# Attention and FFN block: norms and residual moved to GpSimd, the bias of every head pair copied into PSUM

## The chip, the cores and the metric

The kernel runs on one core of a Trainium2 chip. The metric is the device time of one execution in microseconds, median of the runs. Engines are called TensorE (PE in the rows; PEld is its weight load), VectorE (DVE), ScalarE (ACT), GpSimd (POOL) and SyncE (SP, which issues DMAs).

## What is computed

Input x is 8 batches of 256 tokens of 128 features, float32. Layer norms have no gain or shift, eps is 1e-5.

```python
x = x + _layernorm(attn(_layernorm(x)))
x = x + _layernorm(ffn(_layernorm(x)))

def attn(x):                       # 16 heads of 8
    qkv = x @ W_qkv + b_qkv
    ...
    scores = einsum('bihd,bjhd->bhij', q, k) / sqrt(8)
    rel = clip(idxs[:, None] - idxs[None, :] + 128, 0, 256)
    scores = scores + transpose(rel_bias[rel], (2, 0, 1))[None]
    out = einsum('bhij,bjhd->bihd', softmax(scores), v)
    return out @ W_out + b_out

def ffn(x):                        # 128 -> 512 -> 512 -> 512 -> 128, ternary weights, per-output scales
    h = silu(x @ w1 * s1) * (x @ w2 * s2)
    h = gelu(h @ h1 * h1s); h = gelu(h @ h2 * h2s)
    return h @ w3 * w3s
```

## The kernel before

**Number format.** TensorE works in float32r, which keeps fewer bits than float32. Where that matters an operand is split in a high part (rounded) and a low part (the rest), and products of both are added. The table of relative biases lies in SBUF as `raw` (128 x 16 heads x 384, so that every head's bias of a tile is a window), its rounded form as `table_hi`, and for one pair of heads also the rest, `table_lo`.

**Program.** It is written by hand in one queue per engine, with semaphores; nothing is reordered. There are 8 pairs of heads (s = 0 to 7) in each of 8 batches (b = 0 to 7). Token tiles of 128 come in five units of 2, 2, 4, 4 and 4; each unit is normalised (`x_moments`, `inv_std` on GpSimd, `x_normalize`), transposed (`x_T`) and multiplied with the weights of q, k and v (`q_and_k`, `v`).

**Softmax.** The maximum of a row must be known before the exponential. So each pair is multiplied twice: once one batch ahead for the maximum (`max_scores` L1222, 4 matmuls; `max_bias` L1240, 2 matmuls with the identity that add `table_hi`; `maxima` L683 on VectorE), and once transposed for the probabilities (`scores` L1257, 4 matmuls, which also subtract the maximum by an extra row). The bias of this second product is in PSUM before the scores are added: `write_bias` copies the windows of `raw` there, on ScalarE (L1012) for pairs 0, 1, 3, 4, 6, on VectorE (L690) for pairs 2 and 5 (`BY_DVE`). In the last batch VectorE takes 1, 2, 4, 5, 6. For pair 7 (`BY_PE`) nobody copies: `score_bias` (L1276) adds `table_hi` and `table_lo` with 4 matmuls behind the scores. ScalarE's `probabilities` (L1004) is the exponential, and `weighted` (L1285) multiplies two pairs with v. Three PSUM places of two banks rotate: pair i of the scores and pair i of the maxima use place i % 3, so a bias may be written only when `maxima` has read the place (`ms_read`), and a maximum's matmuls may start only when the exponential has read it (`exp_done`).

**The steps of a batch.** In step s of batch b TensorE does the scores of (b, s), the maximum's product of (b+1, s), its bias, for s = 7 the bias matmuls, and then one of the small things for batch b-1: `back` (s 1, 2: weighted heads back to tokens), `heads_T` (s 3), `project` (s 4, L1317: the output projection, P below) and `norm_T` (s 7, L1324: transposes the second norm z into the FFN's input, N below). In step 6 of batches 1 to 4 it also does unit 4's transpose or products, ahead of the maximum's product.

**The norms around the attention**, all of batch b-1 during batch b. VectorE: `attn_moments` (s 4, L709: adds b_out, statistics of y), `residual` (s 5, L719: normalises y in two instructions, adds it to xs, statistics of the sum), `second_norm` (s 6, L731: normalises into z in two instructions), `z_low` (s 7, L739). GpSimd computes each reciprocal root (`inv_std` L514), and between the batches it splits the FFN's weights into parts (`split_weights`, four instructions of 128 x 512 a piece, up to three pieces a batch, L559 to L571).

```python
if s == 5:
    residual(b - 1)
if s == 6:
    second_norm(b - 1)
```

**The FFN** (`ffn`, L1542) follows in four chunks of 512 tokens. Its first part contains the rest of batch 7: `back`, `heads_T`, `project`, and `norm_T(B - 1)` ahead of the last outputs of `layer2`. GpSimd, VectorE and ScalarE split the activations into parts.

Of the kernel before, what the change touches and what calls it, by code (L numbers as in the profile page):

```python
# [4 lines left out]
F32 = mybir.dt.float32  # L5
# [9 lines left out]
P = 128  # L15
# [42 lines left out]
BY_PE = (7,)  # L58
BY_DVE = (2, 5)
LAST_BY_DVE = (1, 2, 4, 5, 6)  # L60
LOW_AT_SLOT = {2 * s + k: 2 * i + k for i, s in enumerate(BY_PE) for k in range(2)}
# [25 lines left out]
def build(nc, x, wq, wk, wv, bqk, brows, bv, wo, bo, ext, w1, s1, w2, s2, h1, h1s, h2, h2s, w3, w3s,  # L87
          ident_in, out):
    ctx = ExitStack()
    with ctx:  # L90
# [49 lines left out]
        rows_at = lo_at + 2 * len(BY_PE) * WIN  # L140
        room = sb("room", [P, max(rows_at + 4 * PAIRS * S, 2 * NK * CH * SLOTS)], F32R)
        table_hi = room[:, hi_at:lo_at].rearrange("p (h c) -> p h c", h=H)
        table_lo = room[:, lo_at:rows_at].rearrange("p (h c) -> p h c", h=2 * len(BY_PE))
# [97 lines left out]
        table_lo_set = sem("table_lo_set")  # L241
# [103 lines left out]
        def by_act(b):  # L345
            return tuple(s for s in range(PAIRS) if s not in BY_PE + by_dve(b))

# [158 lines left out]
        def _(pool):  # L506
# [20 lines left out]

            x_inv_std(0)
# [3 lines left out]
            x_inv_std(1)  # L532
            x_inv_std(2)
            for s in range(PAIRS):
                table_high(s)
                if s == 5:
                    x_inv_std(3)
            for i, s in enumerate(BY_PE):
                pool.wait_ge(table_hi_pool, s + 1)
                nc.gpsimd.tensor_tensor(table_lo[:, 2 * i:2 * i + 2, :], raw[:, 2 * s:2 * s + 2, :],  # L540
                                        table_hi[:, 2 * s:2 * s + 2, :].bitcast(F32),
                                        ALU.subtract).then_inc(table_lo_set, 1)

            x_inv_std(4)

# [48 lines left out]
            inv_std((B - 1) * 2 + NU + 1, TPB)  # L594
            inv_std((B - 1) * 2 + NU + 2, TPB)
# [7 lines left out]
        def _(dve):  # L603
# [24 lines left out]
            def x_normalize(u):  # L628
                first, tiles = UNITS[u]
                dve.wait_ge(rstd_set, u + 1)  # L630
                if u >= 3:
                    dve.wait_ge(xnT_ready, 2 if u == 3 else 4)
# [28 lines left out]
            x_moments(1)  # L661
# [3 lines left out]
            spread_weights(nc.vector.tensor_copy, 0, (0,))  # L665
            dve.wait_ge(brows_in, 16)
# [6 lines left out]
            x_normalize(1)  # L673
            dve.wait_ge(ident_loaded, 16)
            nc.vector.tensor_scalar(minus_ident[:, :], ident[:, :], -1.0, None, ALU.mult).then_inc(minus_set, 1)
            dve.wait_ge(qk_w_in[2], 16)
# [32 lines left out]
            def attn_moments(b):  # L709
# [6 lines left out]
                dve.wait_ge(y_read, b + 1)  # L716
# [937 lines left out]
```

## Time and profile before

| | us |
|---|---|
| median of 3 runs (lowest, highest) | 291.42 (290.83, 292.56) |
| profiled execution: its time | 292.18 |
| profiled execution: span of the profile | 290.4 |

| engine | busy us | share of the span |
|---|---|---|
| TensorE | 268.5 | 92% |
| VectorE | 219.3 | 76% |
| ScalarE | 205.9 | 71% |
| GpSimd | 102.4 | 35% |

The granted clock of TensorE is full in all but the last stretch (mean 0.991). The span can be read in four parts: loading, first norms and the maxima of batch 0 (to 33 us), batches 0 to 6 (to 178), the last batch (to 194), and the FFN (to the end). A busy TensorE does not mean a TensorE at its peak: the duration of a matmul in the rows overlaps the next one's, so costs are taken from start to start.

### The profile page before, as it was taken

The page shows a single profiled execution, that of the slowest core. Times are in us where ns is not written, and L with a number is a line of the kernel's source. Part 1 is how long each engine was busy: PE and PEld are TensorE (multiplying, and loading weights), DVE is VectorE, ACT ScalarE, POOL GpSimd, SP SyncE. Part 2 cuts the span into 40 slices and gives each one's busy share as a digit, 9 for nine tenths or more (in the row PEclk, how much of TensorE's full clock was granted, in tenths as well). Part 3 has the DMA queues.
Part 4 walks back from the last instruction along what each step waited for, and adds up shares of the span by engine and source line. Part 5 has one row for each costly group of instructions (what it writes and reads, how often), then busy time and mean ns, then how long its engine had stood idle before and what let it go on. Part 6 is the DMA issues. An engine that isn't in the chain of part 4 may idle for free.

```text
span 290.4 us, 5171 instructions
## 1 busy us (share of the span) xinstructions
PE 268.5 (92%) x1875; PEld 180.4 (62%) x1875; DVE 219.3 (76%) x442; ACT 205.9 (71%) x316; POOL 102.4 (35%) x107
## 2 busy tenths in 40 slices
PE   7999989899999999999998998899999999999980
PEld 7756645555555554565554554567887888888860
DVE  3489977889789889889889899848556843673674
ACT  2777777776786786885886876777469976896750
POOL 7616000103504305906966957018630202400111
PEclk9999999999999999999999999999999999999996
DMA  6979506232221263470320200000000000010012
GB/s 166 320 238 142 184 11 208 89 83 77 74 76 38 77 207 124 138 224 8 104 81 19 61 1 3 1 3 1 0 2 0 0 0 2 0 36 2 2 36 77
DMA packets 21356, 21.17 MB, mean 73 GB/s; under 512 B 3664, under 2 KB 18768, under 8 KB 21072
## 3 DMA queue, kind: packets, MB, share of 16 engines
q1 hardware_dynamic: 20464, 20.53, 24.8%
q8 instruction: 17, 0.28, 0.4%
q10 hardware_dynamic: 864, 0.27, 0.4%
q14 instruction: 11, 0.09, 0.1%
HBM read 14.90 MB, written 5.64 MB: 71 GB/s over the span
## 4 chain that ended last, share of the span: by engine, by line
PE 60%; DVE 22%; ACT 9%; issue 5%; DMA 1%; POOL 0%; SPq 0%; ACTq 0%; DVEq 0%
PE place L1441 10%; PE place L1442 10%; PE place L1244 8%; DVE mx L685 7%; PE pv L1296 6%; PE place L1236 4%; ACT ring L1008 4%; DVE y_and_z L620 4%; PE place L1270 4%; DVE stats L609 2%; PE place L1195 2%; DVE place L692 2%; ACT place L1015 2%; PE pv L1442 2%; PE pv L1441 2%
## 5 line engine op out<-in xcount | busy, mean ns | idle before, releaser
L685 DVE TENSOR_REDUCE mx<-place 128x4 f32<-128x1024 f32 x64 | 78.1, 1222 | 13.1 <-PE place L1244 11.8
L517 POOL TENSOR_TENSOR rstd<-mv,mhalf 128x2 f32<-128x2 f32 (+1 forms) x26 | 21.0, 809 | 153.0 <-DVE mv L617 153.0
L1008 ACT ACTIVATE ring<-place 128x1024 f32<-128x1024 f32 x64 | 65.6, 1027 | 6.3 <-PE place L1281 3.0
L1244 PE MATMUL place<-room,identr 128*128 128x512 f32 x128 | 46.9, 447 | 0.0
L1015 ACT COPY place<-raw 128x1024 f32<-128x1024 f32 x37 | 37.7, 1022 | 12.2 <-DVE mx L685 11.9
L1441 PE MATMUL place<-room,w_hi 128*128 128x512 f32 (+1 forms) x116 | 44.6, 387 | 0.7 <-DVE room L818 0.7
L1442 PE MATMUL place<-room,w_hi 128*128 128x512 f32 (+1 forms) x116 | 44.0, 382 | 0.0
L818 DVE TENSOR_TENSOR room<-ring,room 128x512 fp32r<-128x512 f32 x32 | 21.4, 690 | 18.5 <-ACT room L1096 18.5
L1296 PE MATMUL pv<-ring,vx 128*9 128x256 f32 x512 | 33.6, 380 | 0.0
L1270 PE MATMUL place<-room 33*128 33x256 f32 x256 | 31.7, 328 | 1.1 <-DVE place L692 1.0
L1236 PE MATMUL place<-room 33*128 33x256 f32 x256 | 28.3, 297 | 2.9 <-ACT ring L1008 2.7
L1270 PEld LDWEIGHTS place<-room 33*128 33x128 f32 x256 | 18.9, 184 | 15.4 <-issue 12.2
L1020 ACT COPY oT<-pv 128x256 f32<-128x256 f32 x32 | 11.8, 370 | 22.2 <-PE pv L1296 22.1
L1236 PEld LDWEIGHTS place<-room 33*128 33x128 f32 x256 | 19.8, 185 | 10.1 <-issue 6.8
L1441 PEld LDWEIGHTS place<-room,w_hi 128*128 128x128 f32 x116 | 21.8, 188 | 5.1 <-DVE room L818 0.9
L1244 PEld LDWEIGHTS place<-room,identr 128*128 128x128 f32 x128 | 19.0, 188 | 8.6
L1442 PEld LDWEIGHTS place<-room,w_hi 128*128 128x128 f32 x116 | 21.8, 188 | 4.1
L692 DVE COPY place<-raw 128x1024 f32<-128x1024 f32 x19 | 23.2, 1225 | 0.6
L1094 ACT ACTIVATE ring<-place,hs 128x512 f32<-128x512 f32 x27 | 18.5, 686 | 5.9 <-PE place L1442 5.9
L1296 PEld LDWEIGHTS pv<-ring,vx 128*9 128x9 f32 x512 | 10.9, 90 | 17.3 <-issue 9.9
L830 DVE SCALAR_TENSOR_TENSOR ring<-place,hs,raw 128x512 f32<-128x512 f32 x16 | 12.0, 750 | 12.0 <-ACT raw L1073 11.8
L1096 ACT CAST room<-ring 128x512 fp32r<-128x512 f32 x32 | 19.9, 621 | 1.0
(141 smaller groups left out, 442.9 us busy)
## 6 DMA issues: line engine op xcount, KB each, us to landing
raw<-ext SPq DMA_DIRECT2D x8, 384.0 KB, 6.9
room<-q_parts SPq DMA_DIRECT2D x48, 64.0 KB
room<-k_parts SPq DMA_DIRECT2D x48, 64.0 KB
w_lo<-h SPq DMA_DIRECT2D x2, 1024.0 KB, 5.2
q_parts<-w_hi SPq DMA_DIRECT2D x4, 256.0 KB, 3.0
k_parts<-w_hi SPq DMA_DIRECT2D x2, 512.0 KB, 3.4
xs<-x SPq DMA_DIRECT2D x3, 256.0 KB, 5.7
w_lo<-w SPq DMA_DIRECT2D x3, 256.0 KB, 2.7
```

The source lines that it names most:

```text
L517: nc.gpsimd.tensor_tensor(rstd[:, at:at + width], mv[:, at:at + width, 1], mhalf[:, 0:width], ALU.pow).then_inc(rstd_set, 1)
L685: nc.vector.tensor_reduce(mx[:, s // RPAIRS, :, :, s % RPAIRS].rearrange("p i k -> p k i"), max_tile(b * PAIRS + s)[:, :, :].rearrange("p ...
L692: nc.vector.tensor_copy(score_tile(i)[:, :, :].rearrange("p k (j n) -> p k j n", j=2), pair_windows(raw[:, :, :], i % PAIRS)).then_inc(bia ...
L818: nc.vector.tensor_tensor(lo, act_f[:, half[c], k, :], hi.bitcast(F32), ALU.subtract).then_inc((a1_lo_set, a2_lo_set)[i], 1)
L1008: nc.scalar.activation(probs[:, s % PRING, :, :, :].rearrange("p k j n -> p (k j n)"), score_tile(b * PAIRS + s)[:, :, :].rearrange("p k n ...
L1015: nc.scalar.copy(score_tile(i)[:, :, :].rearrange("p k (j n) -> p k j n", j=2), pair_windows(raw[:, :, :], i % PAIRS)).then_inc(bias_set, 1)
L1236: mm(max_tile(b * PAIRS + s)[:, half, it * S:(it + 1) * S], rows(q_rows, b, half, s)[:, it * P:(it + 1) * P], rows(k_rows, b, half, s), st ...
L1244: last = mm(max_tile(b * PAIRS + s)[:, half, :], identr[:, :], windows(table_hi[:, 2 * s + half, :], 0, P, 2, S), start=False, stop=True, ...
L1270: last = mm(tile[:, half, j * S:(j + 1) * S], rows(k_rows, b, half, s)[:, j * P:(j + 1) * P], rows(q_rows, b, half, s), start=(s in BY_PE ...
L1296: last = mm(pv[32 * r:32 * r + VC, 0:S], vx[:, b * TPB + j, 4 * g + r, :], probs[:, (2 * g + r // 2) % PRING, r % 2, j, :], start=(j == 0) ...
L1441: mm(o, w, hi, start=first, stop=False)
L1442: done = mm(o, w, lo, start=False, stop=last and exact)
```

## The change

- **Bias.** `BY_PE` and `score_bias` are gone. Pair 7's bias is copied like the others, by VectorE in batches 0 to 6 (`BY_DVE` is 2, 5, 7; written in step 5), by ScalarE in the last batch. `table_lo` is not computed. `table_hi` stays for the maxima.
- **Norms.** GpSimd does `residual` and `second_norm` of every batch, the statistics of the sum stay on VectorE as `x1_moments`, in step 6. GpSimd also normalises units 2, 3 and 4 of x, between the casts of the table.
- **Start.** The moments of unit 1 come behind the normalising of unit 0.
- **FFN.** `project(B - 1)` follows output 2 of `layer1` of chunk 1, where it followed output 1.

```diff
-BY_PE = (7,)
-BY_DVE = (2, 5)
+BY_DVE = (2, 5, 7)
...
@@ GpSimd
+            def residual(b):
+                inv_std(b * 2 + NU + 1, TPB)
+                pool.wait_ge(rstd_set, b * 2 + NU + 1)
+                for t in range(TPB):
+                    last = normalize(y[:, t, :], y[:, t, :], t)
+                last.then_inc(y_norm, 1)
+                pool.wait_ge(y_norm, b + 1)
+                xb = xs[:, TPB * b:TPB * b + TPB, :]
+                nc.gpsimd.tensor_tensor(xb, xb, y[:, :, :], ALU.add).then_inc(x1_set, 1)
+
+            def second_norm(b):
+                inv_std(b * 2 + NU + 2, TPB)
+                pool.wait_ge(rstd_set, b * 2 + NU + 2)
+                if b > 0:
+                    pool.wait_ge(zT_ready, b)
+                for t in range(TPB):
+                    last = normalize(z[:, t, :], xs[:, b * TPB + t, :], t)
+                last.then_inc(z_set, 1)
...
+            table_high(0)
+            table_high(1)
             x_inv_std(2)
-            for s in range(PAIRS):
+            table_high(2)
+            x_normalize(2)
+            for s in range(3, 6):
                 table_high(s)
-                if s == 5:
-                    x_inv_std(3)
-            for i, s in enumerate(BY_PE):
-                pool.wait_ge(table_hi_pool, s + 1)
-                nc.gpsimd.tensor_tensor(table_lo[:, 2 * i:2 * i + 2, :], raw[:, 2 * s:2 * s + 2, :],
...
+            x_inv_std(3)
+            x_normalize(3)
+            table_high(6)
+            table_high(7)
             x_inv_std(4)
+            x_normalize(4)
...
                 if b > 0:
-                    inv_std((b - 1) * 2 + NU + 1, TPB)
-                    inv_std((b - 1) * 2 + NU + 2, TPB)
+                    residual(b - 1)
+                    second_norm(b - 1)
                 for piece in SPLIT_AT[b]:
                     split_weights(piece)
...
@@ VectorE
             x_moments(0)
             dve.wait_ge(qk_w_in[0], 16)
             nc.vector.tensor_scalar(wq_sb[:, :], wq_sb[:, :], scale, None, ALU.mult).then_inc(bq_scaled, 1)
-            x_moments(1)
             x_normalize(0)
             dve.wait_ge(row_zeros, 1)
             dve.wait_ge(bq_scaled, 1)
             spread_weights(nc.vector.tensor_copy, 0, (0,))
+            x_moments(1)
...
-                        if s == 5:
-                            residual(b - 1)
                         if s == 6:
-                            second_norm(b - 1)
+                            x1_moments(b - 1)
...
@@ TensorE
-                    if s in BY_PE and more:
-                        score_bias(b, s)
-                    if s + 1 in BY_PE and not more:
+                    if s + 2 == PAIRS and not more:
 
                         scores(b, s + 1)
-                        score_bias(b, s + 1)
...
-                whole(layer1, 1, exact, (0, 1))
+                whole(layer1, 1, exact, (0, 1, 2))
                 project(B - 1)
-                whole(layer1, 1, exact, (2, 3))
+                whole(layer1, 1, exact, (3,))
```

VectorE's queue in batch 6, from the moments of y to the low part of z, before (`mx<-place` are the maxima of pairs 5, 6 and 7 of the next batch; `y_and_z` is y in the first two rows and z in the last two of it):

```order
L617 TENSOR_SCALAR mv<-mv 128x2 [waits dve_order]
L685 TENSOR_REDUCE mx<-place 128x2x2 [waits ms_ready]
L620 TENSOR_SCALAR y_and_z<-y_and_z,mv,rstd 128x128 [waits rstd_set]
L727 TENSOR_TENSOR xs<-xs,y_and_z 128x256 [waits y_norm]
L609 BN_STATS stats<-xs 128x6 [waits x1_set]
L685 TENSOR_REDUCE mx<-place 128x2x2 [waits ms_ready]
L620 TENSOR_SCALAR y_and_z<-xs,mv,rstd 128x128 [waits zT_ready,rstd_set]
L743 TENSOR_TENSOR z_parts<-misc,z_parts 128x256 [waits z_hi_set]
```

and after:

```order
L646 TENSOR_SCALAR mv<-mv 128x2 [waits dve_order]
L712 TENSOR_REDUCE mx<-place 128x2x2 [waits ms_ready]
L719 COPY place<-raw 128x1024 [waits ms_read]
L712 TENSOR_REDUCE mx<-place 128x2x2 [waits ms_ready]
L638 BN_STATS stats<-xs 128x6 [waits x1_set]
L712 TENSOR_REDUCE mx<-place 128x2x2 [waits ms_ready]
L758 TENSOR_TENSOR z_parts<-misc,z_parts 128x256 [waits z_hi_set]
```

The bias of pair 7 (`place<-raw`) has come in behind the maxima of pair 5, and the statistics of the sum, which stood ahead of the maxima of pair 6, stand behind them; both normalisings and the addition have left.

GpSimd's queue between two batches' weight pieces, after (before, only the two `rstd` rows stood there):

```order
L513 TENSOR_TENSOR rstd<-mv,mhalf 128x2 [waits var_set]
L525 TENSOR_SCALAR y_and_z<-y_and_z,mv,rstd 128x128 [waits rstd_set]
L545 TENSOR_TENSOR xs<-xs,y_and_z 128x256 [waits y_norm]
L525 TENSOR_SCALAR y_and_z<-xs,mv,rstd 128x128 [waits zT_ready,rstd_set]
L588 CAST w_hi<-w_lo 128x512 [waits parts_out4,ffn_w_in3]
```

The weight pieces of a batch now stand behind five more instructions.

TensorE's queue in step 7 of a batch, before:

```order
L1270 MATMUL place<-room 128x256 [waits ms_read]
L1236 MATMUL place<-room 128x256 [waits exp_done]
L1244 MATMUL place<-room,identr 128x512 x2
L1281 MATMUL place<-room,identr 128x512 x4
L1327 MATMUL misc<-ident,y_and_z 128x128 [waits z_set,mrow_set]
```

and after:

```order
L1275 MATMUL place<-room 128x256 [waits bias_set_dve]
L1243 MATMUL place<-room 128x256 [waits exp_done]
L1251 MATMUL place<-room,identr 128x512 x2
L1322 MATMUL misc<-ident,y_and_z 128x128 [waits z_set,mrow_set]
L1275 MATMUL place<-room 128x256 [waits bias_set,mrow_in0]
```

Between the bias of the maxima and the transpose of z the four matmuls are gone; the scores of pair 7 now wait for VectorE's copy.

## Rows read from the trace of the kernel before

**Rows 1.** The page, part 1: busy us, share of the span, instructions.
```profile
PE 268.5 (92%) x1875; PEld 180.4 (62%) x1875; DVE 219.3 (76%) x442; ACT 205.9 (71%) x316; POOL 102.4 (35%) x107
```

**Rows 2.** TensorE's timeline, batches 1 and 2: start, us, what, [idle before].
```profile
65.55 0.71 PE L1320 MATMUL misc<-wo_sb,onT 128*128 128x128 f32 x4
...
69.56 0.74 PE L1244 MATMUL place<-room,identr 128*128 128x512 f32 x2
...
73.40 0.38 PE L1327 MATMUL misc<-ident,y_and_z 128*128 128x128 f32 x2
...
86.17 0.71 PE L1320 MATMUL misc<-wo_sb,onT 128*128 128x128 f32 x4
...
90.67 0.73 PE L1244 MATMUL place<-room,identr 128*128 128x512 f32 x2
...
94.99 0.44 PE L1327 MATMUL misc<-ident,y_and_z 128*128 128x128 f32 x2 [0.35 <-DVE w_hi L640]
...
107.26 0.71 PE L1320 MATMUL misc<-wo_sb,onT 128*128 128x128 f32 x4
```

**Rows 3.** TensorE's timeline, batch 5: projection, bias matmuls, transpose, next projection.
```profile
149.46 0.71 PE L1320 MATMUL misc<-wo_sb,onT 128*128 128x128 f32 x4
...
155.53 1.09 PE L1281 MATMUL place<-room,identr 128*128 128x512 f32 x4
...
157.68 0.41 PE L1327 MATMUL misc<-ident,y_and_z 128*128 128x128 f32 x2 [1.06 <-DVE y_and_z L620]
...
169.67 0.71 PE L1320 MATMUL misc<-wo_sb,onT 128*128 128x128 f32 x4
```

**Rows 4.** VectorE's timeline over the same part of batch 5.
```profile
147.81 1.23 DVE L692 COPY place<-raw 128x1024 f32<-128x1024 f32 x1
...
151.54 1.22 DVE L685 TENSOR_REDUCE mx<-place 128x4 f32<-128x1024 f32 x1
...
152.68 0.60 DVE L620 TENSOR_SCALAR y_and_z<-y_and_z,mv,rstd 128x128 f32<-128x128 f32 x2
...
153.77 0.49 DVE L609 BATCH_NORM_STATS2 stats<-xs 128x6 f32<-128x128 f32 x2
...
154.65 1.22 DVE L685 TENSOR_REDUCE mx<-place 128x4 f32<-128x1024 f32 x1
...
155.78 1.74 DVE L620 TENSOR_SCALAR y_and_z<-xs,mv,rstd 128x128 f32<-128x128 f32 x2
```

**Rows 5.** GpSimd's timeline, batch 5: the root of the second norm.
```profile
154.82 0.70 POOL L517 TENSOR_TENSOR rstd<-mv,mhalf 128x2 f32<-128x2 f32 x1 [2.38 <-DVE mv L617]
```

**Rows 6.** GpSimd's groups by line and shape: busy us, mean ns of one, idle before.
```profile
L569 POOL TENSOR_SCALAR w_hi<-w_lo 128x512 fp32r<-128x512 f32 x10 | 15.0, 1505 | 0.9
...
L561 POOL TENSOR_TENSOR w_lo<-w_lo,w_hi 128x512 f32<-128x512 f32 x11 | 14.1, 1284 | 0.9
...
L559 POOL CAST w_hi<-w_lo 128x512 fp32r<-128x512 f32 x11 | 6.8, 620 | 0.0
...
L525 POOL CAST room<-raw 128x768 fp32r<-128x768 f32 x8 | 6.3, 830 | 0.9 <-DMA raw<-ext 0.9
...
L540 POOL TENSOR_TENSOR room<-raw,room 128x768 fp32r<-128x768 f32 x1 | 1.8, 1809 | 0.1
```

**Rows 7.** TensorE's timeline: start, end of batch 0, last batch, FFN.
```profile
7.31 0.41 PE L1169 MATMUL misc<-ident,xn 128*128 128x128 f32 x2 [0.80 <-DVE xn L620]
...
54.12 0.51 PE L1236 MATMUL place<-room 33*128 33x256 f32 x4 [0.77 <-ACT ring L1008]
...
190.73 1.05 PE L1296 MATMUL pv<-ring,vx 128*9 128x256 f32 x16
...
220.12 0.71 PE L1320 MATMUL misc<-wo_sb,onT 128*128 128x128 f32 x4 [0.69 <-ACT onT L1024]
```

**Rows 8.** ScalarE's timeline, last batch.
```profile
189.00 1.94 ACT L1008 ACTIVATE ring<-place 128x1024 f32<-128x1024 f32 x2 [1.57 <-PE place L1270]
```

More of the change, by code:

```diff
@@ L55 @@
 SLOT_HEAD = [s + HALF * k for s in range(PAIRS) for k in range(2)]
-BY_PE = (7,)
-BY_DVE = (2, 5)
+BY_DVE = (2, 5, 7)
 LAST_BY_DVE = (1, 2, 4, 5, 6)
-LOW_AT_SLOT = {2 * s + k: 2 * i + k for i, s in enumerate(BY_PE) for k in range(2)}
 def windows(ap, start, step, count, width):
@@ L345, in by_act @@
         def by_act(b):
-            return tuple(s for s in range(PAIRS) if s not in BY_PE + by_dve(b))
+            return tuple(s for s in range(PAIRS) if s not in by_dve(b))
         BLANKS = (2, 2, 2, 6, 6)
@@ L526, in table_high, with normalize, x_normalize @@
                                       raw[:, 2 * s:2 * s + 2, :]).then_inc(table_hi_pool, 1)
+            def normalize(dst, src, t, at=0):
+                return nc.gpsimd.tensor_scalar(dst, src, mv[:, at + t, 0:1], rstd[:, at + t:at + t + 1],
+                                               ALU.subtract, ALU.mult)
+            def x_normalize(u):
+                first, tiles = UNITS[u]
+                pool.wait_ge(rstd_set, u + 1)
+                if u >= 3:
+                    pool.wait_ge(xnT_ready, 2 if u == 3 else 4)
+                for t in range(tiles):
+                    last = normalize(x_norm[u][:, t, :], xs[:, first + t, :], t, first)
+                last.then_inc(xn_set, 1)
+            def residual(b):
[15 more added lines that the diff above has]
+                last.then_inc(z_set, 1)
             x_inv_std(0)
@@ L593, in _ @@
             gate_parts(2)
-            inv_std((B - 1) * 2 + NU + 1, TPB)
-            inv_std((B - 1) * 2 + NU + 2, TPB)
+            residual(B - 1)
+            second_norm(B - 1)
             gate_parts(3)
@@ L716, in attn_moments, with x1_moments @@
                 dve.wait_ge(y_read, b + 1)
+                if b > 0:
+                    dve.wait_ge(z_set, b)
                 moments(lambda t: y[:, t, :], TPB, b * 6 + base + 2)
[L719 to L727 removed]
+            def x1_moments(b):
                 dve.wait_ge(x1_set, b + 1)
                 moments(lambda t: xs[:, b * TPB + t, :], TPB, b * 6 + base + 4)
[L731 to L737 removed]
             def z_low(b):
@@ L748, in _ @@
                 if s == 0:
-                    x_normalize(2)
                     keep_v(0)
@@ L863, in _ @@
             layer_low(1, 0, (0, 1))
-            residual(B - 1)
+            x1_moments(B - 1)
             layer_low(1, 0, (2, 3))
-            second_norm(B - 1)
             layer_low(0, 1)
@@ L1271, in scores @@
                                   rows(k_rows, b, half, s)[:, j * P:(j + 1) * P], rows(q_rows, b, half, s),
-                                  start=(s in BY_PE and j == 0), stop=False, skip_group_check=True)
-                if s not in BY_PE:
-                    last.then_inc(st_ready, 1)
-            def score_bias(b, s):
-                if b == 0:
-                    pe.wait_ge(table_lo_set, BY_PE.index(s) + 1)
-                for half in range(2):
-                    for part in (table_hi[:, 2 * s + half, :], table_lo[:, LOW_AT_SLOT[2 * s + half], :]):
-                        last = mm(score_tile(b * PAIRS + s)[:, half, :], identr[:, :], windows(part, 0, P, 2, S),
-                                  start=False, stop=True, skip_group_check=True)
+                                  start=False, stop=False, skip_group_check=True)
                 last.then_inc(st_ready, 1)
@@ L1356, in _ @@
                 for s in range(PAIRS):
-                    if more or s not in BY_PE:
+                    if more or s < PAIRS - 1:
                         scores(b, s)
```

33 lines of the change are left out of this document (3 added, 30 removed).

## The prediction

> **What bounds the kernel now.** I read the page's busy shares first, then TensorE's timeline around the eight attention batches, then VectorE's and GpSimd's over the same stretch, and last the groups of GpSimd instructions. TensorE is busy for 92% of the span [rows 1], so the first question is whether the bias matmuls of pair 7, which the change removes from it, stand where TensorE has no slack. They don't. In batch 5 the last thing before the transpose of the second norm (L1327) is the group of four bias matmuls at 155.53 (1.09 us, of which the last 0.1 overlap, so about 0.95 of path), and then the transpose waits 1.06 us for VectorE's normalised tile [rows 3]. The 0.95 us before that wait is no cost as long as the wait stands. Batch 2 shows the same shape with a shorter wait, and batch 3 repeats it [rows 2].
>
> A batch is therefore two stretches. From the transpose (N) to the projection (P, L1320) TensorE works nearly without a gap: 157.68 to 169.67 is 12.0 us [rows 3]; batch 2 needs 94.99 to 107.26, 12.3, and batch 1 needs 73.40 to 86.17, 12.8, with small waits for exponentials of pair 7 in them [rows 2, 3]. From P to N a chain decides: moments, reciprocal root, normalising, residual, moments, reciprocal root, normalising. It takes 7.85 us in batch 1, 8.82 in batch 2, 8.22 in batch 5 [rows 2, 3]. What the change is worth in the loop is what it does to this chain.
>
> **The chain after the change.** VectorE loses the residual (152.68 to 153.77, 1.09 us) and the second normalising (155.78, 1.74 us for two) [rows 4]. That second number holds contention: the same two instructions take 0.60 at 152.68. It gains the bias of pair 7, put behind the maxima of pair 5: 1.23 us [rows 4]. It then does the maxima of pair 6, and only then the moments of the residual sum; the second normalising follows on GpSimd behind them. By the rows of batch 5:
> - maxima of pair 5 start at 151.54 and end at 152.76; the bias waits for that end, so it runs from 152.80; the next instruction starts 1.13 later, at 153.93 (maxima of pair 6); 1.14 later the moments, 155.07.
> - From the first statistics to GpSimd's root is 1.05 (153.77 to 154.82), the root takes 0.70, and 0.09 goes by to an instruction that depends on it [rows 4, 5]. GpSimd starts normalising at 156.91.
> - Two normalisings of length d, then 0.16 to TensorE: N at 157.07 + 2d, against 157.68 now. So batches 5 and 6 change by 2d - 0.61.
> - In batches 2 to 4 TensorE has a product of 1 us ahead of pair 6, so the maxima of pair 6 start at 91.45, 0.78 after L1244 at 90.67; N comes at 91.45 + 1.14 + 1.05 + 0.70 + 0.09 + 2d + 0.16 = 94.59 + 2d against 94.99: 2d - 0.40. In batch 1, 69.56 + 0.78 + 3.14 + 2d = 73.48 + 2d against 73.40: 2d + 0.08 [rows 2].
>
> The first half (root, two normalisings, one addition on GpSimd) lies beside VectorE's bias and maxima: 0.70 + 0.09 + 2d + 0.09 + 0.76, starting just behind the start of the maxima at 151.54, must be done by 155.07. With d = 0.56 it is done at about 154.4; the cover is gone above d = 0.85 or so.
>
> **d is not in the trace.** GpSimd has run no subtract-multiply with two scalars per partition. The nearest rows [rows 6]: a one-operation TENSOR_SCALAR of 512 columns takes 1505 ns; the two-input one 1284 at 512 and 1809 at 768, hence 2.05 ns a column and 0.24 fixed; the cast 620 at 512 and 830 at 768, hence 0.82 a column and 0.20 fixed. Below, a normalising that streams like the cast takes 0.20 + 128 x 0.00082 = 0.30. Above, it is no longer than the whole 512-column row, 1.5. I take the TENSOR_SCALAR row, same opcode: 0.24 + 128/512 x 1.265 = **0.56 us**, an estimate. The addition of 256 columns is 0.24 + 256 x 0.00205 = 0.76.
>
> The Trainium skill (GPSIMD Engine Reference, Engine selection) says that one-input elementwise work on GpSimd runs at roughly line rate and two-input work about half as fast as on VectorE. The cast agrees with line rate, but the TENSOR_SCALAR row, which has one input too, is the slowest of all per column. By the page the normalising would cost what the cast does, and the sum would be that of rival A below, -1.0 instead of +2.1.
>
> **The sum, against the profiled execution** (span 290.4, time 292.18; the median is 291.42, 0.76 lower, so I add the same sum to the median):
> - Chain, batches 1 to 6: (2d + 0.08) + 3 (2d - 0.40) + 2 (2d - 0.61) = 12d - 2.34 = **+4.4** at d = 0.56.
> - The stretch from N to P: pair 7's exponential no longer follows a matmul bias, so the waits right behind N go: 12.8 to 12.0 once and 12.3 to 12.0 three times, **-1.6**. Zero to -1.9.
> - Batch 0: no chain there. TensorE waits 0.77 us for an exponential after the bias matmuls, at 54.12 [rows 7]; the bias by VectorE pushes the maxima of pairs 6 and 7 back by about 0.8, and ScalarE's exponential of pair 7 with them, so of the 0.95 + 0.77 about 0.4 is left: **-0.4** (0 to -0.95).
> - Last batch: ScalarE must write pair 7's bias between the exponentials of pairs 5 and 6, which now run back to back from 189.00 [rows 8]; TensorE's product of pair 4 and 5's probabilities (190.73) [rows 7] stands behind the scores of pair 7 in its queue, and the last exponential behind that. Bias 0.95, scores 0.5, and the removed matmuls had stood at the same place: **+0.95** (0.5 to 1.3).
> - FFN: the projection moves one output later. Now it waits 0.69 us for ScalarE's copy, at 220.12 [rows 7]; 1.8 us later the copy is long there: **-0.7**. The residual and second norm go to GpSimd here as well. VectorE's moments stand behind the same four subtractions as before, so this chain starts no later; it costs 4d + 0.76 = 3.0 us of GpSimd for 1.7 of VectorE, and seven outputs of about 1.8 us of TensorE lie between the projection and its transpose now, less one then. I cost it at nothing; a d of 1.2 would use the cover up.
> - Start: moments of unit 1 now follow the first normalising, so that one needn't wait. TensorE's first transpose stands at 7.31 behind a wait of 0.80 [rows 7], the most that can go. But unit 1's normalising comes 0.4 later, and ScalarE's two takes follow it: **-0.5** (0 to -0.8).
> - The low part of the table (one instruction, 1.8 us [rows 6]) and units 2 to 4's normalising (12 instructions) on GpSimd: nothing, for GpSimd idles here; the tables must be there for TensorE's bias of the maxima, and 4d = 2.2 us more ahead of tables 3 and 6 leaves them over a microsecond early. Without that cover each 1 us more on GpSimd would stand in the path once. VectorE's relief at the start is worth nothing either, TensorE having no gap there.
>
> 4.4 - 1.6 - 0.4 + 0.95 - 0.7 - 0.5 = **+2.1 us**, or 292.18 + 2.1 = 294.3 for this execution and **293.5** for the median. In terms of d it is 12d - 4.6.
>
> **Rivals.**
> A, GpSimd streams (d about 0.30): 12 x 0.30 - 4.6 = -1.0, 290.4. For it: the cast rows. Against: the TENSOR_SCALAR row, one operation and already 3 times the cast per column.
> B, GpSimd is slow (d of 0.9 or more, as two operations and two pointer operands may cost): 12 x 0.9 - 4.6 = +6.2, 297.6; then the first half of the chain shows as well, and in batches 4 and 5 three weight pieces on GpSimd come between the norms and the next root.
> C, the other side: TensorE keeps its freed time. That is so if the transpose finds its tile ready: the second normalising would have to be done before 156.5 in batch 5, which is d below 0 by the chain above, unless the moments of the sum go ahead of what I have put before them or the maxima get shorter without contention. Price: eight times 0.95 and the 1.2 us at start and FFN, less nothing else: -8.8, 282.6. Against: the order of VectorE's instructions, which the row after pair 6 fixes.
> D, contention: GpSimd's normalising beside VectorE's instructions with two ports slows one or the other, as the 1.74 us pair shows [rows 4]. In the chain VectorE then runs maxima and bias, which never stretched; only the 170 ns additions to the variance could wait. Twelve waits of up to 0.6: +3, so 296.5.
>
> **How the numbers follow.** Forecast 0.50 (d from 0.42 to 0.8: 291.9 to 296.4), A 0.22, B 0.10, C 0.06, D 0.12. Predicted 293.5. The range leaves out C, B's upper half and the gains beyond A: 290.0 to 297.0. A change of 0.5% (1.5 us) is about what can be told from none: the border lies at 289.96 and 292.88. Faster: C and a tenth of A's weight with larger gains at the start, 0.10. Same: most of A and a third of the forecast (d below 0.5), 0.35. Slower: the rest, 0.55.
>
> **What would show it.** Right: in TensorE's timeline no L1281, N behind a wait of 1.5 to 2.5 us for GpSimd in each batch 1 to 6; P to N 8.7 in batch 5 and 9.5 in batch 2; N to P 12.0 in all; GpSimd's normalising rows at 0.56; the last batch 1 us longer. Wrong: no wait at N (C); normalising rows near 0.3 (A) or 0.9 (B); L646 or the moments on VectorE well over 0.2 each (D). If P to N is as written and N to P is not 12.0, the stretch was not TensorE's.

## The result: 329.34 us, slower by 13%

| | us |
|---|---|
| before: median of 4 runs (lowest, highest) | 291.64 (290.83, 292.56) |
| after: median of 4 runs (lowest, highest) | 329.34 (327.76, 336.08) |
| ratio after to before, 95% interval | 1.127 (1.120, 1.133) |
| profiled execution of after: time, span | 336.08, 334.2 |
| mean granted clock of TensorE, before and after | 0.991, 0.854 |

The forecast was 293.5 and the range ended at 297.0. The profiled execution of after is its slowest, 6.7 us above the median; the other four on record (one of them not among the table's four) took 327.8 to 330.5 us at clocks of 0.875 to 0.880, so the loss and the low clock stand in every run, and its stretches below are longer than a typical run's. This is the page of after, parts 1 and 2:

```profile
PE 297.3 (89%) x1843; PEld 191.5 (57%) x1843; DVE 204.7 (61%) x397; ACT 209.7 (63%) x317; POOL 142.6 (43%) x158
...
PEclk9999998597599579599679559755899999999996
```

TensorE executes 32 matmuls fewer than before and is busy for 29 us more [rows 1]. The second line says how: the granted clock, which stood at 0.991 before, drops to 5 tenths again and again through the attention batches. TensorE's timeline of batch 1 shows where. P is now L1315 (before L1320), N is L1322 (before L1327), and the groups to compare with are [rows 2]:

```profile
69.42 0.71 PE L1315 MATMUL misc<-wo_sb,onT 128*128 128x128 f32 x4
...
76.26 0.74 PE L1251 MATMUL place<-room,identr 128*128 128x512 f32 x2
79.44 0.46 PE L1322 MATMUL misc<-ident,y_and_z 128*128 128x128 f32 x2 [2.44 <-POOL y_and_z L525]
...
80.98 1.22 PE L1251 MATMUL place<-room,identr 128*128 128x512 f32 x2
82.13 1.90 PE L1291 MATMUL pv<-ring,vx 128*9 128x256 f32 x16
...
95.91 1.05 PE L1291 MATMUL pv<-ring,vx 128*9 128x256 f32 x16
96.89 0.71 PE L1315 MATMUL misc<-wo_sb,onT 128*128 128x128 f32 x4
```

The wait at N is there, 2.44 us long and ended by GpSimd, as forecast. Behind it the two bias matmuls of L1251 take 1.22 us instead of 0.74, and the sixteen of L1291 1.90 instead of 1.05. N to P is 17.5 us; forecast was 12.0. The same stretch in slices of 4 us, core 0; after the window come its length, the busy time of PE, PEld, DVE, ACT and POOL (with instructions), the granted clock, the DMA share and GB/s:

```profile
76.00:80.00 4.00, 1.56 (x12) 0.80 (x11) 1.98 (x6) 2.46 (x4) 3.00 (x5) 0.96 0.20 55
80.00:84.00 4.00, 4.00 (x27) 1.74 (x28) 2.16 (x3) 2.24 (x3) 3.74 (x4) 0.50 0.26 78
84.00:88.00 4.00, 4.00 (x22) 2.71 (x20) 1.84 (x2) 1.76 (x3) 0.63 (x1) 0.50 0.15 29
88.00:92.00 4.00, 4.00 (x27) 1.75 (x26) 1.79 (x4) 2.08 (x3) 0.00 (x0) 0.50 0.10 39
92.00:96.00 4.00, 4.00 (x30) 2.73 (x33) 2.04 (x4) 3.46 (x5) 0.00 (x0) 0.84 0.04 11
```

TensorE did 1.56 us of work in 4, and then ran at a granted clock of 0.50, which is 1.2 of its 2.4 GHz, for some 13 us, though it had no gap in them. The Trainium skill (TensorE: Matmul & The Clock Gate, Part 1) calls the half rate the default, released by activity. By that rule it is idleness that costs the clock, not load, and the fall in these rows agrees. That the half rate then lasted through 13 us of matmuls without a gap is not explained by it.

The group of waits at N over the whole run (us in total, times, longest; the seventh is in the FFN), and what GpSimd did there in batch 4 (it answers to [rows 4, 5], which are of batch 5):

```profile
PE misc L1322 <- POOL y_and_z L525: 16.8, 7, 2.8
```

```profile
152.00 0.73 POOL L513 TENSOR_TENSOR rstd<-mv,mhalf 128x2 f32<-128x2 f32 x1 [7.24 <-DVE mv L646]
152.83 1.58 POOL L525 TENSOR_SCALAR y_and_z<-y_and_z,mv,rstd 128x128 f32<-128x128 f32 x2
154.50 0.73 POOL L545 TENSOR_TENSOR xs<-xs,y_and_z 128x256 f32<-128x256 f32 x1
157.22 0.71 POOL L513 TENSOR_TENSOR rstd<-mv,mhalf 128x2 f32<-128x2 f32 x1 [1.99 <-DVE mv L646]
158.03 1.57 POOL L525 TENSOR_SCALAR y_and_z<-xs,mv,rstd 128x128 f32<-128x128 f32 x2
```

A normalising takes d = 0.78 us (1.57 for two), not 0.56. By the prediction's own formula, 12d - 4.6, that is +4.8 us, 296.2 for the median: inside the range, and an eighth of the 37.7 us that were lost. The question for the experiments was whether the clock is the rest, and what lets it fall: the wait, the matmuls that are gone, or GpSimd.

### The profile page after: what moved, and what is told of

It reads as the page before. It is cut to its first block, busy times and chain, and to the rows that moved or that the text cites. A ratio compares the mean times of both kernels' runs of the same rounds, so it can differ in the third digit from the quotient of the medians.

```text
span 334.2 us, 5122 instructions
## 1 busy us (share of the span) xinstructions
PE 297.3 (89%) x1843; PEld 191.5 (57%) x1843; DVE 204.7 (61%) x397; ACT 209.7 (63%) x317; POOL 142.6 (43%) x158
## 4 chain that ended last, share of the span: by engine, by line
PE 60%; DVE 14%; POOL 12%; issue 8%; ACT 4%; DMA 1%; POOLq 0%; DVEq 0%; ACTq 0%
PE place L1251 9%; PE pv L1291 9%; PE place L1433 7%; PE place L1434 7%; POOL y_and_z L525 7%; PE place L1275 6%; DVE mx L712 5%; PE place L1243 4%; POOL rstd L513 4%; PE misc L1302 4%; DVE place L719 2%; PE place L1202 2%; DVE stats L638 2%; PE pv L1169 1%; POOL xs L545 1%
## 5 line engine op out<-in xcount | busy, mean ns | idle before, releaser
L1251 PE MATMUL place<-room,identr 128*128 128x512 f32 x128 | 53.8, 505 | 0.0
L1022 ACT COPY place<-raw 128x1024 f32<-128x1024 f32 x38 | 38.7, 1020 | 17.1 <-DVE mx L712 17.1
L1291 PE MATMUL pv<-ring,vx 128*9 128x256 f32 x512 | 45.6, 488 | 0.0
L1275 PE MATMUL place<-room 33*128 33x256 f32 x256 | 39.1, 393 | 3.4 <-ACT place L1022 1.6
L1275 PEld LDWEIGHTS place<-room 33*128 33x128 f32 x256 | 24.1, 234 | 22.5 <-issue 14.3
L719 DVE COPY place<-raw 128x1024 f32<-128x1024 f32 x26 | 31.8, 1226 | 0.9
L1243 PE MATMUL place<-room 33*128 33x256 f32 x256 | 30.7, 322 | 1.6 <-ACT ring L1015 1.6
L1251 PEld LDWEIGHTS place<-room,identr 128*128 128x128 f32 x128 | 21.8, 214 | 9.9 <-issue 3.1
L1243 PEld LDWEIGHTS place<-room 33*128 33x128 f32 x256 | 23.3, 220 | 7.2 <-issue 3.2
L1291 PEld LDWEIGHTS pv<-ring,vx 128*9 128x9 f32 x512 | 12.4, 102 | 24.7 <-issue 20.7
```

Of the source, the lines that this page charges most:

```text
L719: nc.vector.tensor_copy(score_tile(i)[:, :, :].rearrange("p k (j n) -> p k j n", j=2), pair_windows(raw[:, :, :], i % PAIRS)).then_inc(bia ...
L1022: nc.scalar.copy(score_tile(i)[:, :, :].rearrange("p k (j n) -> p k j n", j=2), pair_windows(raw[:, :, :], i % PAIRS)).then_inc(bias_set, 1)
L1243: mm(max_tile(b * PAIRS + s)[:, half, it * S:(it + 1) * S], rows(q_rows, b, half, s)[:, it * P:(it + 1) * P], rows(k_rows, b, half, s), st ...
L1251: last = mm(max_tile(b * PAIRS + s)[:, half, :], identr[:, :], windows(table_hi[:, 2 * s + half, :], 0, P, 2, S), start=False, stop=True, ...
L1275: last = mm(tile[:, half, j * S:(j + 1) * S], rows(k_rows, b, half, s)[:, j * P:(j + 1) * P], rows(q_rows, b, half, s), start=False, stop= ...
L1291: last = mm(pv[32 * r:32 * r + VC, 0:S], vx[:, b * TPB + j, 4 * g + r, :], probs[:, (2 * g + r // 2) % PRING, r % 2, j, :], start=(j == 0) ...
```

## The experiments

Blank matmuls below are matmuls on a tile of zeros into a PSUM place that is free then; nobody reads their result. Before has them already in its last batch. The ratio of each experiment is to runs of before made beside it; their median was 292.03 us for experiments 1 to 4, 291.45 for 5, 7, 10 and 11, and 292.17 for 6, 8, 9 and 12, so a difference between the medians of two experiments is uncertain by up to 0.7 us.

**1. The wait filled.** On the kernel after:

```diff
+                    if s == 7 and b == 0:
+                        pe.wait_ge(oT_set, GROUPS - 1)
+                        stream(pv, blank, blank, 8)
                     if s == 7 and b > 0 and more:
+                        pe.wait_ge(oT_set, b * GROUPS + GROUPS - 1)
+                        stream(pv, blank, blank, 13)
```

> The kernel after, with TensorE's wait in front of the transpose of the second norm filled: 13 matmuls on blank data (results unused) in each of batches 1 to 6, placed behind the weighted products of pair 6 and held until these are through, and 8 of them near the end of batch 0. No other engine's work changes, and the chain through GpSimd is as long as in the kernel after. Theory (clock): the waits of 2.4 to 2.8 us let the granted clock fall to 0.50 for the 12 us behind them, and that is most of the loss. Then TensorE's mean granted clock is back above 0.97, N to P is 12 to 13 us in every batch in place of 14 to 17.5, and the time is 291.4 + 4.8 = 296 us (294 to 300). Rival 1 (latency or contention: GpSimd's and VectorE's operations are slower and TensorE waits for them): nothing is gained, 325 to 330 us. Rival 2 (the clock falls whatever TensorE does in the wait, for instance by what the other engines draw): the clock stays near 0.87 and the time near 328.

Measured: 304.7 us, ratio to before 1.046 (1.041, 1.050), clock 0.977. Work that nobody needs takes 24.6 us off the kernel. N to P is 12.0 us in all of batches 1 to 5. The size was missed by 9 us: the clock still fell at the start of batch 7 and in the last batch (P to N 14.0 there, 10.1 before), and the chain is longer than 12d - 4.6 has it (below).

**2. The bias moved to VectorE, the norms around the attention on VectorE as before.** On the kernel after, so its last batch, start and projection stay as in the change:

```diff
                         if s == 5:
+                            residual(b - 1)
                         if s == 6:
-                            x1_moments(b - 1)
+                            second_norm(b - 1)
```

> The kernel after, with the residual and the second norm back on VectorE (GpSimd keeps the reciprocal roots and the start's normalising); pair 7's bias stays with VectorE and no bias is on TensorE. Theory (clock): what opens the wait is mostly that TensorE's 0.95 us of bias matmuls are gone and VectorE's 1.25 us of bias are in the chain, not GpSimd. Wait in front of the transpose: 1.06 + 0.95 + 1.25, about 3.3 us at most in batch 5, clock falls behind it as in the kernel after; time 315 to 332 us. Rival (GpSimd's slow normalising is the cause): the wait is under 1.5 us, the clock holds, 289 to 294 us.

Measured: 322.7 us, single runs from 313.88 (clock 0.927) to 331.4 (0.869); even the fastest is 22 us above before. The wait stands at N with no GpSimd in it, ended by VectorE:

```profile
185.31 0.64 PE L1321 MATMUL misc<-ident,y_and_z 128*128 128x128 f32 x2 [3.08 <-DVE y_and_z L630]
```

So GpSimd's slow normalising is not needed for the loss.

**3. Only the residual and the second norm moved to GpSimd; TensorE keeps pair 7's bias.** On the kernel before:

```diff
-                        if s == 5:
-                            residual(b - 1)
                         if s == 6:
-                            second_norm(b - 1)
+                            x1_moments(b - 1)
```

> The kernel before, with only the residual and the second norm moved to GpSimd (TensorE keeps the bias matmuls of pair 7, the start is that of before). Theory: two normalisings of 0.78 in place of 0.30 to 0.87, twice in the chain: the first half on GpSimd is done about 1 us later than the maxima of pair 6, N comes at about 158.4 in place of 157.7 in batch 5, wait in front of it 1.8 us in place of 1.06. Time by the chain alone: 291.4 + 6 x 0.7 = 295.6. If a wait of 1.8 us also costs the clock, as 2.4 us do, 310 to 325. Rival (GpSimd's part is most of the loss): above 320.

Measured: 305.72 us, 1.045 (1.039, 1.050), clock 0.965. Waits at N of 1.5 us in batches 1 to 4. Two of the four (batches 1 and 4) were followed by N to P of 12.0 us, the others by 13.5 and 16.1. This lies between the two cases of the expectation: a wait of 1.5 us costs the clock some of the time. In batch 6 a wait of 1.94 us cost nothing (9.0 us from N to P, as before).

**4. Pair 7's bias by ScalarE.** On the kernel after, with the norms back on VectorE and GpSimd's weight pieces behind the norm:

```diff
-BY_DVE = (2, 5, 7)
+BY_DVE = (2, 5)
+                if SPLIT_AT[b]:
+                    pool.wait_ge(z_set, b)
                 for piece in SPLIT_AT[b]:
                     split_weights(piece)
```

> No bias on TensorE, but pair 7's bias is written by ScalarE, not VectorE, in every batch; residual and second norm on VectorE as before; GpSimd's weight pieces start only when the second norm of the batch is done, so that they don't run beside it. Theory (clock): the wait in front of the transpose is 1.06 + 0.95 - 1.1 (the 1.74 us pair back at 0.6), about 1 us, the clock holds at 0.98 or more, and the time is 284 to 291 us. If ScalarE becomes what the batch waits for (its bias of 0.95 us ahead of the exponentials), 290 to 296. Rival (any bias off TensorE thins its activity and costs the clock, whatever the wait): 300 or more.

Measured: 298.51 us, single runs from 293.46 (clock 0.972) to 304.79 (0.929). The theory of the expectation (284 to 291 us, clock 0.98 or more) missed. P to N is short, 7.1 us in batch 5 against 8.2 [rows 3], and yet the clock was lost once behind batch 5's transpose and once in the last batch:

```profile
152.47 0.74 PE L1252 MATMUL place<-room,identr 128*128 128x512 f32 x2
153.75 0.41 PE L1323 MATMUL misc<-ident,y_and_z 128*128 128x128 f32 x2 [0.54 <-DVE y_and_z L632]
154.28 0.63 PE L1276 MATMUL place<-room 33*128 33x256 f32 x4
155.24 0.80 PE L1244 MATMUL place<-room 33*128 33x256 f32 x4 [0.32 <-ACT ring L1016]
155.96 1.22 PE L1252 MATMUL place<-room,identr 128*128 128x512 f32 x2
```

Here the clock fell behind a wait of 0.54 us, with another of 0.32 just after it; in batches 2 and 3 a wait of 0.54 us was followed by 12.6 us from N to P, as in experiment 11 with the clock held. In before, waits of 1.06 at the same place cost nothing [rows 3]; but there 1.09 us of bias matmuls stood just ahead. The length of one wait alone does not decide. That work missing on TensorE can cost the clock with a short wait is the rival of this expectation, though its 300 us or more was not reached by the median either.

**5. Everything filled.** As 1, with 24 blanks in batches 5 and 6, and in the last batch

```diff
                     if s + 2 == PAIRS and not more:
+                        pe.wait_ge(oT_set, b * GROUPS + 2)
+                        stream(pv, blank, blank, 14)
                         scores(b, s + 1)
```

> As e1_fill, with the two stretches in which its granted clock still fell filled as well: 24 blank matmuls in place of 13 in batches 5 and 6 (1.6 us of wait were left there), and 14 in the last batch, ahead of the scores of pair 7, where TensorE waits 1.8 us for ScalarE's bias. Theory (clock): the granted clock is 1.00 from the first batch to the end, the last P to N falls from 14.0 to about 10.5 us, and the time is 296 to 299.5 us: what is left over the kernel before is the chain through GpSimd at 0.78 us a normalising. Rival (what is left of e1_fill's loss is in waits, not in the clock): no gain, 303 to 306.

Measured: 299.65 us, 1.026 (1.023, 1.029), clock 0.993; the expectation ended at 299.5 and had the last P to N at 10.5 us, where it is 11.3. The page, and the chain's end in batch 1, where TensorE streams through most of the wait:

```profile
PEclk9999999999999999999999999999999999999997
```

```profile
72.39 1.70 PE L1169 MATMUL pv<-blank 128*128 128x256 f32 x13
75.00 0.41 PE L1322 MATMUL misc<-ident,y_and_z 128*128 128x128 f32 x2 [0.91 <-POOL y_and_z L525]
```

VectorE, ScalarE and GpSimd have exactly the instructions of after. By the medians the clock is 29.7 us of the loss of 37.7, and what is left, 8.0 us, is what the change costs with the clock held.

**6. Fewer blanks.** 6 in place of 13 and 24, otherwise as 5.

> The kernel after with 6 blank matmuls before the transpose in batches 1 to 6 (e6_fill_all has 13 and 24), the rest as e6_fill_all: about 0.8 us of the wait of 2.4 to 2.8 us filled, 1.7 and 2.0 left. Theory (the clock depends on how much of the wait is work): between the two, the clock falls behind some of the waits and not behind others, 302 to 318 us. Rival (any work at all in the wait is enough): 299.7. Other rival (a wait over 1 us is always too long): 322 or more.

Measured: 313.43 us, single runs from 305.84 (clock 0.968) to 314.79 (0.931). Two waits of practically the same length, and the slice of 4 us behind each:

```profile
75.06 0.66 PE L1322 MATMUL misc<-ident,y_and_z 128*128 128x128 f32 x2 [1.74 <-POOL y_and_z L525]
...
102.96 0.41 PE L1322 MATMUL misc<-ident,y_and_z 128*128 128x128 f32 x2 [1.75 <-POOL y_and_z L525]
```

```profile
76.00:80.00 4.00, 4.00 (x28) 1.62 (x26) 2.33 (x3) 2.16 (x4) 3.79 (x3) 0.50 0.20 63
...
104.00:108.00 4.00, 4.00 (x40) 2.34 (x40) 3.33 (x4) 3.33 (x5) 3.55 (x3) 1.00 0.20 59
```

The first was followed by 17.4 us from N to P, the second by 12.0. At such a wait it goes either way. Kernels that lose the clock often also scatter from run to run: 3% here, 4% in experiments 4 and 7, 6% in 2, against 0.2% in experiment 5. It is no certain sign: experiment 8 loses the clock in its last batch and scatters by 0.15%.

**7. A long wait with nothing else of the change.** The kernel before, with five spare additions on VectorE ahead of each second normalising:

```diff
+                for k in range(5 if b < B - 1 else 0):
+                    dve.wait_ge(z_spare, 5 * b + k)
+                    nc.vector.tensor_tensor(z[:, :, :], xs[:, b * TPB:b * TPB + TPB, :], xs[:, b * TPB:b * TPB + TPB, :],
+                                            ALU.add).then_inc(z_spare, 1)
```

> The kernel before, with nothing taken from TensorE: only five additions of 256 columns more on VectorE (into the second norm's own tile, which the norm overwrites) ahead of each second normalising of batches 1 to 7, about 2.0 us. GpSimd does no more than before. Theory (a long wait of TensorE alone costs the clock): the wait before the transpose is 2.4 us in batches 1 to 4 and about 3 in 5 and 6; the clock falls behind most of them, time 310 to 330 us. Rival (it takes the missing bias matmuls, or GpSimd's work, as well): clock 0.98, 291.4 + 6 x 2.0 = 303 us, 300 to 305.

Measured: 329.55 us, 1.125 (1.120, 1.129). The additions came out longer than expected, 3.8 us for the five in batch 1, so the waits at N are 3.6 to 4.7 us. TensorE's bias matmuls are all there, and the clock falls as in after:

```profile
73.01 1.10 PE L1288 MATMUL place<-room,identr 128*128 128x512 f32 x4
77.94 0.66 PE L1334 MATMUL misc<-ident,y_and_z 128*128 128x128 f32 x2 [3.83 <-DVE y_and_z L621]
```

In the profiled execution (span 340.1, 49.7 more than before) P to N grew by 22.9 us over batches 1 to 6; the other 26.8 came behind the waits: N to P is 13.5 to 17.5 us in batches 1 to 5. Neither the missing matmuls nor GpSimd's part is needed. This delays by more than after does, so it shows that a wait suffices, not how short one may be.

**8. The last batch alone.** The kernel before, with pair 7's bias by ScalarE there:

```diff
+        def by_pe(b):
+            return BY_PE if b + 1 < B else ()
                         scores(b, s + 1)
-                        score_bias(b, s + 1)
```

> The kernel before with one part of the change, in the last batch alone: pair 7's bias is written by ScalarE, TensorE's four bias matmuls go. The prediction gave this part +0.95 us (292.4); with it in e6_fill_all the last P to N was 11.3 us against 10.1 before. Theory: the clock falls here too, as it did in e1_fill and e5_act_bias (last P to N 14.0 and 15.1 us), and the time is 295 to 297 us. Rival (the clock fell there only because earlier batches had left TensorE with gaps): 292 to 293.

Measured: 295.99 us, 1.013 (1.010, 1.015); last P to N 14.1 us. At full clock (experiment 5) it was 11.3, against 10.1 before: the term of the prediction, +0.95, was nearly right at +1.1, and the clock adds 2.8 on top. All earlier batches are as before, so the expectation's rival, that earlier gaps prepare the fall, is refuted.

```profile
191.63 0.50 PE L1273 MATMUL place<-room 33*128 33x256 f32 x4 [1.80 <-ACT place L1018]
...
192.49 1.47 PE L1299 MATMUL pv<-ring,vx 128*9 128x256 f32 x16
...
196.01 1.90 PE L1299 MATMUL pv<-ring,vx 128*9 128x256 f32 x16
```

**9. The bias part priced at full clock.** Experiment 2 with 16, 26 and 14 blanks.

> e3_bias_only (norms on VectorE, bias by VectorE) with its waits filled by 16 blank matmuls in batches 1 to 4, 26 in 5 and 6, 14 in the last. It prices the bias on VectorE at full clock, without GpSimd's norms. Theory: what the change costs at full clock is nearly all VectorE's 1.25 us of bias with what it pushes back (P to N 9.0 to 10.4 us as in e3_bias_only), not GpSimd's norms: 298 to 301 us, as e6_fill_all (299.65). Rival (the two parts add up): 294 to 296.

Measured: 298.15 us, 1.020 (1.018, 1.023), 6.0 above the runs of before beside it; for experiment 5 that is 8.2. So most of the 8 us is there without GpSimd's residual and second norm. P to N over batches 1 to 6 is 7.3 us longer than before with the norms on VectorE, and 7.95 with bias and norms moved. In experiment 3, the norms alone, it is 7.9, with some of the clock lost. The two parts do not add up: GpSimd's first normalising and addition run beside VectorE's bias, and in after GpSimd then waits 1.99 us for VectorE (the row at 157.22, in the section on the result).

**10. The weight pieces held, nothing else.** The kernel before, with the weight pieces held as in experiment 4.

> The kernel before; GpSimd's pieces of the FFN weights start only when the second norm of the batch is done. Theory: the 1.74 us pair of the second normalising on VectorE falls to 0.6, which takes about 1 us from the chain in batches 5 and 6 and less in 2 to 4 (where the transpose hardly waits): 288.5 to 290.5 us. Rival (it is not GpSimd that stretches the pair): 291 to 292.

Measured: 291.31 us, 0.999 (0.997, 1.001). The pair of [rows 4] that took 1.74 us takes 0.59, so it is GpSimd's pieces that stretch it:

```profile
155.66 0.59 DVE L622 TENSOR_SCALAR y_and_z<-xs,mv,rstd 128x128 f32<-128x128 f32 x2
```

P to N falls by 1.15 us in batches 5 and 6 each. And N to P rises from 12.0 to 12.9 in batch 5: TensorE now waits for ScalarE's exponentials (4.8 us over the run, before 2.7). From batch 1 to 6 P to N is 3.7 us shorter in all and N to P 3.1 us longer, so most of the gain was given back. The time is the rival's (291 to 292), but its reason is refuted: GpSimd does stretch the pair.

**11 and 12. A version about 1% faster than before.** Experiment 4 has the short chain and takes 0.95 us of work from TensorE; it lacked only the clock. First with 5 blanks ahead of the transpose, 4 in batch 0 and 14 in the last batch:

> e5_act_bias with 5 blank matmuls in its remaining wait before the transpose (0.5 us) in batches 1 to 6, 4 at the end of batch 0 and 14 in the last batch ahead of the scores of pair 7. Theory (clock): e5_act_bias had the shortest chain of all (P to N 7.1 to 8.1 us against 7.9 to 8.8 before) and lost it to two stretches at half clock (N to P 18.1 in place of 12.6 once, last P to N 15.1); with the clock held it runs in 298.3 - 5.5 - 4.5 = 288 us (285.5 to 290). Rival: the clock falls in e5_act_bias for another reason than the work missing on TensorE, and the time stays at 293 to 305.

Measured: 288.88 us, 0.989 (0.986, 0.992). Then with before's start and its last batch, where TensorE keeps the bias:

```diff
+        def by_pe(b):
+            return BY_PE if b + 1 == B else ()
+                        stream(pv, blank, blank, 5)
-                    if s in BY_PE and more:
-                        score_bias(b, s)
```

> The kernel before with: pair 7's bias by ScalarE in batches 0 to 6 and still by TensorE in the last, GpSimd's weight pieces held until the second norm of the batch is done, and 5 blank matmuls (4 in batch 0) in front of the transpose of the second norm. It is e7_act_fill with the last batch (P to N 11.3 us) and the start as they were before (10.1). Theory: 288.9 - 1.1 = 287.8 us, 287 to 289. Rival (the last batch's gain is used up by the waits behind it in the FFN): 288.9.

Measured: 288.50 us, 0.987 (0.984, 0.989). The intervals of the two overlap; that the second is better is not shown. Batch 5's transpose in the second:

```profile
152.16 0.73 PE L1249 MATMUL place<-room,identr 128*128 128x512 f32 x2
152.72 0.74 PE L1167 MATMUL pv<-blank 128*128 128x256 f32 x5
153.43 0.41 PE L1332 MATMUL misc<-ident,y_and_z 128*128 128x128 f32 x2
```

No wait is left, 7.07 us from P to N; and behind it ScalarE is next, as in experiment 10, with 12.9 us from N to P.

## Why the prediction was wrong

**The step that failed** is the pricing of the waits, in "The sum, against the profiled execution". Each wait at N was put into the sum at its own length, and the stretch from N to P was taken as 12.0 us "in all", from rows that had been recorded at full clock. The clock had no term, no rival and no place in the range. The prediction itself named a wait of 1.5 to 2.5 us as what would show it right; it had the wait and missed what follows from it. After against experiment 5, which differ by the blanks alone, from the starts of P and N in the two profiled executions:

| stretch | after | with blanks | difference |
|---|---|---|---|
| start to P of batch 1 | 69.42 | 65.50 | 3.9 |
| P to N, batches 1 to 6 | 60.1 | 58.6 | 1.5 |
| N to P, batches 1 to 5 | 82.9 | 60.0 | 22.9 |
| N to P, batch 6 | 14.1 | 9.0 | 5.1 |
| P to N, last batch | 14.3 | 11.3 | 3.0 |

Together 36.4 us, against 36.3 between the spans (334.2 and 297.9). The first row is the end of batch 0, where the clock fell at about 56 us behind waits of only 0.86 and 0.46 us, in the place of the bias matmuls:

```profile
53.06 0.50 PE L1275 MATMUL place<-room 33*128 33x256 f32 x4 [0.86 <-DMA room<-mrow]
54.01 0.50 PE L1243 MATMUL place<-room 33*128 33x256 f32 x4 [0.46 <-ACT ring L1015]
```

By the medians the difference between the two kernels is 29.7 us.

The prediction's first question was whether the bias matmuls stand where TensorE has no slack, and its answer, that a wait for VectorE follows them, was right. What it did not ask is what the same matmuls do there: they keep TensorE at work while a chain on the other engines runs, and without them the wait is longer by their length.

**The other terms**, at full clock (experiment 5 against before, by the spans 297.9 and 290.4):

| term | forecast, d = 0.56 | same formula, d = 0.78 | measured |
|---|---|---|---|
| P to N, batches 1 to 6 | +4.4 | +7.0 | +7.95 |
| N to P, batches 1 to 5 | -1.6 | -1.6 | -1.7 |
| batch 0 and start | -0.9 | -0.9 | 0.0 |
| last batch | +0.95 | +0.95 | +1.1 |
| FFN | -0.7 | -0.7 | +0.6 |

The measured terms add to 7.95 and the spans differ by 7.5; the missing -0.4 lies behind the last transpose.

- **d**, the second thing mis-sized, was taken from a one-operation row of 512 columns, scaled down. The real instruction, with two operations and two scalars per partition, takes 797 ns for 128 columns (the 16 on y). The Trainium skill (GPSIMD Engine Reference, Engine selection) has one-input work at roughly line rate, which the prediction turned into 0.30; this trace disagrees with it by a factor of 2.7.
- **The chain** is the formula in batches 1 to 3: P to N grew by 1.65, 1.17 and 1.17 against 2d + 0.08 = 1.64 and 2d - 0.40 = 1.16. In batch 5 it grew by 0.4 more, because VectorE's small addition to the variance stretched beside GpSimd's weight pieces, 0.57 us in place of 0.17. That is rival D's mechanism, once in each of batches 5 and 6 and not twelve times:

```profile
154.93 0.57 DVE L646 TENSOR_SCALAR mv<-mv 128x2 f32<-128x2 f32 x1
```

- **Batch 0 and start**: in batch 0 TensorE's scores wait 0.86 us for the row maxima's DMA in after (above), but what releases TensorE behind them is still the exponential of pair 7. It starts at 52.92 us with the blanks and at 52.95 in before. VectorE's bias pushes the maxima back, ScalarE's next copy waits 0.78 us for them, and that uses up all of the freed time, where the prediction left 0.4 us of it. At the start the first transpose came earlier in after (6.55 against 7.31), but by 30.7 us the lead was gone (a product for the maxima starts at 30.74 against 30.70).

```profile
51.97 1.02 ACT L1022 COPY place<-raw 128x1024 f32<-128x1024 f32 x1 [0.78 <-DVE mx L712]
52.92 1.02 ACT L1015 ACTIVATE ring<-place 128x1024 f32<-128x1024 f32 x1
```

- **FFN**: the wait at the projection did go, as forecast, but 1.42 us at the last transpose took its place, for GpSimd. Two things were wrong there. The last two normalisings took 3.29 us in place of 1.57 (one of them 2.23, in after too), while VectorE ran five subtractions in a row (3.10 us from 236.49). And the cover of "seven outputs" was thinner than thought: GpSimd's part is 1.58 + 0.74 + 3.29 = 5.6 us, which is just the prediction's limit (a d of 1.2), and yet TensorE waits. With the norms on VectorE (experiment 9) that wait is gone, and the stretch between the last two transposes is 0.96 us shorter than before. So GpSimd's part, which the prediction put at nothing, cost 1.6 us. That VectorE's subtractions stretch the normalising (rival D's mechanism) is read from these rows; no run isolates it.

```profile
237.87 3.29 POOL L525 TENSOR_SCALAR y_and_z<-xs,mv,rstd 128x128 f32<-128x128 f32 x2
```

- **Rivals**: A fell with d; B had the right side and, at d = 0.78, nearly the right size of the chain, but nothing of the clock; C's condition, no wait at N, was not met in after. Experiments 11 and 12 meet it by another way, and get 2.6 and 3.7 us of its 8.8; part of the rest went to TensorE's waits for ScalarE (N to P 12.9 us in batch 5).
- The closing test, "if N to P is not 12.0, the stretch was not TensorE's", drew the wrong line: N to P was TensorE's all through, at half clock. (P to N was not as written either, 9.5 us in batch 5 where the prediction had 8.7.)

## What to carry to other kernels

Before taking work off a TensorE that is 92% busy, ask what fills its queue while a chain on the other engines runs. If that was the work, the wait that takes its place costs its own length, and here anything from nothing to 5.5 us more for the 12 us of work behind it; read the granted clock in short slices before trusting a duration. Where a wait can't be shortened, blank matmuls in it are the cheapest test of this, and sometimes the remedy: here 24.6 us for five lines. Runs of one kernel that scatter by several per cent, together with their clock, can be a sign of it.

## What the runs showed of the hardware

- The granted clock fell, in part or all of N to P, behind each of the waits of 2.2 us and more ahead of the transpose, behind waits of 1.4 to 1.9 us in some cases and not in others, and once behind one of 0.54 us with others close by. It then stayed there through some 13 us of gapless matmuls at the longest (80 to 93 us in after). What exactly decides was not settled.
- A GpSimd subtract-multiply with two scalars per partition takes 0.78 to 0.80 us for 128 columns (the last in the FFN took 2.23, beside VectorE's subtractions of 512 columns), VectorE 0.34 for the same (L622 in experiment 10).
- VectorE's instructions stretch beside GpSimd's four-instruction weight pieces: the pair of normalisings from 0.60 to 1.74 us, the additions of 256 columns from 0.43 to 0.76 (mean of the five in batch 1 of experiment 7), the two-column addition from 0.17 to 0.57. The maxima (1.22) and the bias copy (1.23) never stretched.
